# Experts stage: a second accumulator for the odd blocks, merged by one adding transfer

## What is computed

```
probs = softmax(x @ router_weight)               # 1024 tokens, 8 experts
top 2 experts of each token, local_probs = probs where chosen, else 0
y = x @ w1[e]; g = silu(y1) * y2; o = g @ w2[e]  # 256 -> 2 x 352 -> 256
out[token] = sum over its two experts of local_probs[token, e] * o
x = x + out
```

## Time and profile before

| | us |
|---|---|
| median of 3 runs (lowest to highest) | 821.13 (819.25 to 827.23) |
| the profiled execution's own time | 814.34 |
| its span, first to last instruction | 812.5 |
| busy: TensorE / VectorE / ScalarE / GpSimd | 659.7 / 496.9 / 360.0 / 305.9 |
| experts phase in the span, about | 655.6 to 812.5 |

### The profile page before, as it was taken

One profiled execution on the slowest core, in us unless ns is written; L12 is line 12 of the kernel. 1 busy time (PEld: TensorE's weight loads), 2 busy tenths in 40 slices (PEclk: granted clock), 3 DMA queues, 4 the chain that ended last, 5 costly groups with the idle time before them and its releaser, 6 DMA issues. The chain is left out here.

```text
span 812.5 us, 16811 instructions
## 1 busy us (share of the span) xinstructions
PE 659.7 (81%) x6073; PEld 504.1 (62%) x6073; DVE 496.9 (61%) x1359; ACT 360.0 (44%) x979; POOL 305.9 (38%) x433
## 2 busy tenths in 40 slices
PE   4999999999999777459934888788999651999991
PEld 3777777877877666345413676467878541677660
DVE  2777777777776799673497743358878636233320
ACT  1445455455544666444665624226665411222220
POOL 2254564564541677510000121037464211355552
PEclk9999999999999999868975799999999975899996
DMA  9532232332210000057000546091000030233332
GB/s 279 196 75 59 76 78 58 76 77 62 72 27 1 2 3 3 2 157 268 16 0 0 208 156 240 21 390 65 2 3 2 1 104 15 47 53 60 61 47 26
DMA packets 30082, 62.85 MB, mean 77 GB/s; under 512 B 5713, under 2 KB 20433, under 8 KB 27569
## 3 DMA queue, kind: packets, MB, share of 16 engines
q1 hardware_dynamic: 25584, 55.65, 21.1%
q0 software_dynamic: 4416, 6.13, 4.8%
HBM read 56.62 MB, written 5.14 MB: 76 GB/s over the span
## 5 line engine op out<-in xcount | busy, mean ns | idle before, releaser
L433 ACT ACTIVATE prob<-s_sb,negm 128x257 f32<-128x257 f32 x128 | 66.2, 517 | 93.5 <-DVE negm L643 93.5
L383 POOL TENSOR_SCALAR bias<-dist,cst 128x257 f32<-128x257 f32 x128 | 59.9, 486 | 100.6 <-DVE dist L630 90.8
L639 DVE CUSTOM_DVE_ANT_0 s_sb<-psum,bias 128x257 f32<-128x257 f32 x128 | 49.4, 423 | 52.7 <-PE psum L511 49.3
L489 PE MATMUL psum<-ctxT,shared 128*128 128x257 f32 x256 | 61.5, 383 | 0.0
L2342 PE MATMUL psum<-ex_w,ex_rT 128*128 x184 | 60.8, 475 | 0.6 <-ACT ex_rT L2266 0.6
L497 PE MATMUL psum<-shared,ctxT 128*128 128x256 f32 x256 | 60.4, 379 | 0.0
L2231 POOL DMA_INDIRECT out<-ex_o,ex_target x23 | 36.4, 1582 | 53.2 <-DMA out<-ex_o,ex_target 29.2
L497 PEld LDWEIGHTS psum<-shared,ctxT 128*128 128x128 f32 x256 | 48.5, 189 | 6.8
L1605 POOL TENSOR_TENSOR wn<-wn,cst 128x1 f32<-128x1 f32 x8 | 4.7, 588 | 124.7 <-DVE wn L1732 124.7
L511 PE MATMUL psum<-kT,qbd 64*128 64x257 f32 x256 | 48.6, 429 | 2.3 <-DVE mx L639 2.1
L489 PEld LDWEIGHTS psum<-ctxT,shared 128*128 128x128 f32 x256 | 46.6, 192 | 5.7 <-issue 0.3
(11 more groups left out here) (350 smaller groups left out, 1642.9 us busy)
## 6 DMA issues: line engine op xcount, KB each, us to landing
ctxT<-in_ctx_T SPq DMA_DIRECT2D x32, 257.0 KB
ex_w<-in_w SPq DMA_DIRECT2D x1, 5632.0 KB, 16.5
kpos<-in_kpos SPq DMA_DIRECT2D x32, 128.5 KB
msk<-in_mask SPq DMA_DIRECT2D x32, 128.5 KB
near_turned<-in_ctx_T_tiles SPq DMA_DIRECT2D x4, 1028.0 KB, 7.4
ff_used_up<-in_ctx_T_tiles SPq DMA_DIRECT2D x4, 1028.0 KB, 7.3
near_rows<-in_ctx_tiles SPq DMA_DIRECT2D x4, 1024.0 KB, 7.6
ff_used_up<-in_ctx_tiles SPq DMA_DIRECT2D x4, 1024.0 KB, 6.9
```

The costliest lines, as they stand in the source:

```text
L383: nc.gpsimd.tensor_scalar(bias[n % 2][:, g, :], dist[n % 2][:], c.slope[:, g:g + 1], 1.0, ALU.mult, ALU.mult).then_inc(bias_ready, 1)
L433: nc.scalar.activation(prob[n % 2][:, g, :], s_sb[n % 2][:, g, :], ACT.Exp, bias=negm[:, b, g:g + 1], accum_out=esum[t % 2][:, b, g:g + 1]) \
L489: ins = nc.tensor.matmul(kv[m][:, 0:SK], w["xa_k"][:, k, P * m:P * m + P], ctxT[n % BT][:, k, :], start=(k == 0), stop=(k == KT - 1))
L639: nc.vector.tensor_tensor_reduce(s_sb[n % 2][:, g, :], sc[g % 2][:, 0:SK], bias[n % 2][:, g, :], 1.0, float("-inf"), ALU.add, ALU.max, mx[ ...
```

## The change

Scatters of even blocks still add into `out`; those of odd blocks add into a second tensor in memory, `odd_blocks`, of the same shape. It must be zero first: GpSimd sets an SBUF tile of 128 x 2304 floats to zero as its first instruction of the phase, and SyncE's queue stores it (1.18 MB), between the store of x and that of `xn`. Each parity has its own semaphore, so scatter(j) waits for scatter(j - 2) instead of scatter(j - 1), and the reuse of an `o` tile waits for the count of its own parity. Behind the last scatters GpSimd waits for both semaphores and issues one direct transfer from memory to memory that adds the 1024 rows of `odd_blocks` (1 MB, as 128 rows of 8 KB) to `out`, and waits for it.

```
+        added, merged, zeros_kept = [esem("added_even"), esem("added_odd")], esem("merged"), esem("zeros_kept")
+        zeros, zeros_set = sb("zeros", [P, (T_ALL + P) * D // P]), esem("zeros_set")
 ...
                 sp.dma_start(out[0:T_ALL, :].rearrange("(t p) d -> p t d", p=P), x[:]).then_inc(x_kept, 16)
+                sp.wait_ge(zeros_set, 1)
+                sp.dma_start(a["odd_blocks"].rearrange("(p t) d -> p (t d)", p=P), zeros[:]).then_inc(zeros_kept, 16)
                 sp.wait_ge(xn_ready, NT // 2)
 ...
             def _(pool):
+                nc.gpsimd.memset(zeros[:], 0.0).then_inc(zeros_set, 1)
                 pool.wait_ge(veps_ready, 1)
 ...
                 def scatter(j):
                     pool.wait_ge(o_ready, j + 1)
-                    at_least(pool, added, 16 * j)
+                    at_least(pool, added[j % 2], 16 * (j // 2))
                     nc.gpsimd.indirect_dma_start(
-                        out, bass.IndirectOffsetOnAxis(target[:, j:j + 1], 0), o[j % RING][:], None,
-                        compute_op=ALU.add).then_inc(added, 16)
+                        (out, a["odd_blocks"])[j % 2], bass.IndirectOffsetOnAxis(target[:, j:j + 1], 0), o[j % RING][:],
+                        None, compute_op=ALU.add).then_inc(added[j % 2], 16)
 ...
                 pool.wait_ge(x_kept, 16)
+                pool.wait_ge(zeros_kept, 16)
 ...
-                pool.wait_ge(added, 16 * MB)
+                pool.wait_ge(added[0], 16 * ((MB + 1) // 2))
+                pool.wait_ge(added[1], 16 * (MB // 2))
+                nc.gpsimd.dma_start(out[0:T_ALL, :].rearrange("(p t) d -> p (t d)", p=P),
+                                    a["odd_blocks"][0:T_ALL, :].rearrange("(p t) d -> p (t d)", p=P),
+                                    accum_op=ALU.add, max_dma_last_dim=4096).then_inc(merged, 16)
+                pool.wait_ge(merged, 16)
 ...
                 def weigh_block(j):
-                    at_least(act, added, 16 * (j - RING + 1))
+                    at_least(act, added[j % 2], 16 * ((j - RING) // 2 + 1))
 ...
+    views["odd_blocks"] = nc.dram_tensor("odd_blocks", (T_ALL + P, D), F32).ap()
```

More of the change, by code:

```diff
@@ L2203, in experts @@
         gT_full, gT_done = esem("gT_full"), esem("gT_done")
-        weight_ready, o_full, o_ready, added = esem("weight_ready"), esem("o_full"), esem("o_ready"), esem("added")
+        weight_ready, o_full, o_ready = esem("weight_ready"), esem("o_full"), esem("o_ready")
+        added, merged, zeros_kept = [esem("added_even"), esem("added_odd")], esem("merged"), esem("zeros_kept")
+        zeros, zeros_set = sb("zeros", [P, (T_ALL + P) * D // P]), esem("zeros_set")
         with nc.Block() as block:
```

## The result

| | us | ratio to the kernel before, 95% interval |
|---|---|---|
| kernel before, 9 runs | 820.88 (818.97 to 827.23) | |
| kernel after, 9 runs | 815.92 (812.37 to 816.65) | 0.9944 (0.9921 to 0.9966) |
| kernel after, timed once more beside before | 816.02 against 818.73 | 0.9972 (0.9954 to 0.9990) |

The change makes the kernel faster by 2 to 5 us, 0.3 to 0.6%, which is no change by the 1% bound of the prediction. The profiled execution took 816.45 us (span 814.6).

A forecast was written before the change was run, and what follows sets the result against it. The string of scatters, each waiting for the last one's landing, was taken to bound the end, 8.0 us behind. Scatters 10.5 us earlier, then 0.73 and a merge of 8.8: -1.0 us, 821.13 to 820.1; range 814 to 829.

The forecast's parts named there:

- the 1% bound of the prediction: The smallest difference from no change that this kernel's measurement was taken to tell: 1%, 8.2 us.
- The wait goes, TensorE's 4.22 us is the pace: Experts phase: without scatter(j)'s wait for scatter(j - 1), TensorE paces blocks; last scatter lands 10.5 us earlier.
- `o` ready to scatter, 0.6 us: End of experts phase: time from a ready o tile to its scatter's start, taken from 757.12 - 756.55 = 0.57.
- Landing to merge, 0.73 us: After the last scatter's landing: GpSimd passes its waits and starts the merge 0.73 us later, at 797.9.
- The merge, 8.8 us: Kernel's end: 6.6 us of data at 0.100 engine-us a KB plus 2.2 fixed, fully on the path.
- Front at nothing: Phase start: memset of 2.0 us hidden in GpSimd's 3.7 us idle, zeros' store of 3.4 us covered; no cost.
- The base: Sum made against the profiled execution, 814.34 us; its difference carried to the runs' median, 6.8 us above, 821.13.
- 1: Rival at the end: the merge runs like a plain copy; -4.6 us, 816.5; chance 0.14.
- 3: Rival at the end: add not overlapped within an engine, merge 19.3 us; +9.5 us, 830.6; chance 0.12.
- 4: Rival in the scatters: issue and queue, not the wait, set the 4.5 us; +9.5 us, 830.6; chance 0.06.
- 5: Rival at the front: late start by slow memset or contended store of xn; +0.7 to +3 us; chance 0.04.
- Rival 2: At the end: the merge runs at a scatter's average rate, 12.4 us; +2.6 us, 823.7; chance 0.16.

The follow-up runs named there:

- the half merge: The kernel after with a merge of the first 512 rows only (128 rows of 4 KB); profile only, 6.1 us from issue to landing.
- the second profile: The kernel before, unedited, timed against itself and profiled again: 819.09 against 818.48 us, ratio 0.9997, span 818.1 us.
- front_only: The kernel before with only the memset, the store of zeros and GpSimd's wait for it: 817.72 us, ratio 0.9983 to the kernel before.

## Why the prediction was right, step by step

Forecast 820 (814 to 829), same; measured 815.9. The range and the class held, and the mechanism is the one that was named.

- **The wait goes, TensorE's 4.22 us is the pace:** right. Gain forecast 10.5 us against one profile; 10.9 against that profile (101.94 to 91.05).
- **`o` ready to scatter, 0.6 us:** it is 0.27. I paired two rows of different blocks. The scatter at 757.12 is block 12's, whose `o` tile had been ready for 4.8 us; the ScalarE row at 756.08 is block 13's tile, which was scattered at 761.78. The 0.57 between them is no wait at all; what that scatter waited for was the landing 0.79 us before it.
- **Landing to merge, 0.73 us:** it is 0.29, for the cause shown above: the merge carries the wait for the even scatters.
- **The merge, 8.8 us:** 8.4 and 8.8. The split holds as a division of time: the engines move data for 6.4 us of it, at a share of 1.00 and 0.098 engine-us a KB, where 6.6 and 0.100 were forecast, and 2.0 us lie outside, where 2.2 were. Part of this is luck. The 0.100 came from 0.4 us of a scatter at a share of 1.22, and I divided it by 16 engines as if the share were 1; that row's own 195 GB/s gives 1049 / 195 = 5.4 us and a merge of 7.6. At full load the merge runs at 0.080 and 217 GB/s, and its slow first packets (802.4 to 803.2, a share of 1.46 for 67 GB/s) bring the average back to 0.098. So as a sum of a fixed part and a part by bytes the split is another: by the half merge 3.8 us fixed and 4.6 a megabyte. The issue is 1.00, not 1.55.
- **Front at nothing:** right; memset 2.02 us against 2.0 forecast. The store of zeros took 5.2 us from issue to landing, against about 3.4 plus the queue before it, and landed at 665.0, still 0.9 us before `xn` was issued.
- **The base:** the step that was off. I carried the gain over from one profile, which was an uncommon execution (router at the higher clock, a short string), and noted 6.8 us between it and the median without asking what they were. Against the second profile, with its string 0.6 us longer, the same steps give -1.6, not -1.0; with the two gaps and the merge as measured they give the -2.7 of the table above. Of the 5.0 us between the two medians of the first timing, this leaves 2.3 that no profile shows.
- **Rivals:** 1 (the merge like a copy) would have been -4.6 us and was measured as a copy, 4.9 us; the add is not one. 3 falls by the profile after already (8.4 us, where it decided from 18 on), 4 by the profile after, 5 by `front_only`. Rival 2 put the merge at 12.4 us and fell with the profile.
- **What no rival named:** that the 0.73 us behind a landing (0.75 with the entry at L70), which I used as a constant in three places, was itself the thing to remove. With up to 0.48 us less a block the string keeps up with TensorE, and the second accumulator has 1.8 us left to win, 92.87 against its 91.05, for a merge of 8.8.

## What to carry to other kernels

When a chain repeats "landing, gap, next issue", ask what the gap is made of before buying a second buffer to hide the landing: here the gap was the larger saving for its price. Where an instruction has several waits, find out which one it carries itself, and let that be the one that comes last; on GpSimd's scatters it was worth up to 0.48 us each, and 9 us in all. And profile the kernel before twice when its profile and its median differ by more than the effect you forecast.

## What the runs showed of the hardware

- A transfer on GpSimd starts 0.27 to 0.29 us after a late wait that it carries, and 0.75 to 0.80 us after one in an instruction ahead of it.
- An adding transfer of 1 MB from memory to memory takes 8.4 to 8.8 us, the same one without the add 4.9; at full load 0.080 against 0.042 engine-us a KB, over the whole data time 0.098 against 0.046. Both went in 256 packets of 4 KB.
- GpSimd issues the merge of 1 MB in 0.66 us as a copy and in 1.00 with an add, an indirect adding transfer of 128 rows in 1.55 to 1.64.
- The router's 32 matmuls of one kernel took 5.17 us in one execution and 7.0 in another, at a granted clock of 0.69 and 0.50. Why the clock was higher in the one is not shown.
